# Where the whole-array products of a quad of attention stand: between its scores and its sums

## The reference, cut to what matters

```
x = x + 0.5 * ffn(layernorm(x))          # 8 experts, top 2 of the gate, three ReLU layers of 128x128
x = x + attention(layernorm(x))
x = x + 0.5 * ffn(layernorm(x))          # the same weights again

def attention(x):                        # 16 query heads of 64, ONE key and ONE value head of 64
    q = x @ Wq + bq                      # (8, 512, 16, 64)
    k = x @ Wk + bk;  v = x @ Wv + bv    # (8, 512, 64) each
    w = softmax(q k^T / 8)               # over the 512 keys
    return (w @ v as (8, 512, 1024)) @ Wo + bo
```

## Time and profile before

| | us |
|---|---|
| median of 3 runs (lowest, highest) | 1103.29 (1102.97, 1105.31) |
| the profiled execution, its own time | 1103.85 |
| its span, first to last instruction | 1102.1 |
| TensorE busy | 1040.5 (94%) |
| VectorE, GpSimd, ScalarE busy | 807.5, 693.6, 612.6 |

### The profile page before, as it was taken

The page is one execution under the profiler, slowest core; times in us unless marked ns, Lnnn a source line. Parts: engine busy times, 40 slices in busy tenths (PEclk is TensorE's granted clock), DMA queues, the critical chain, the costliest instruction groups (busy, mean ns, idle before and its releaser), DMA issues.

```text
span 1102.1 us, 15666 instructions
## 1 busy us (share of the span) xinstructions
PE 1040.5 (94%) x5703; PEld 627.2 (57%) x5703; DVE 807.5 (73%) x1023; ACT 612.6 (56%) x867; POOL 693.6 (63%) x370
## 2 busy tenths in 40 slices
PE   4799997679999999999999999999999999998996
PEld 2567885346555655554565555555565455667883
DVE  6879997757756766777587668666577648699994
ACT  4495554436644654564465457457565476675551
POOL 4365556347775786587578567575678666654652
PEclk9899999879999999999999999999999999999998
DMA  5630520000001001000010010001100103513412
GB/s 158 184 105 23 205 101 10 10 1 21 22 23 39 21 22 40 21 21 21 21 40 22 21 40 21 21 21 35 26 21 22 40 23 97 191 58 95 168 47 77
DMA packets 36339, 59.38 MB, mean 54 GB/s; under 512 B 10502, under 2 KB 23847, under 8 KB 36263
## 3 DMA queue, kind: packets, MB, share of 16 engines
q1 hardware_dynamic: 36192, 58.35, 17.6%
q10 hardware_dynamic: 70, 0.02, 0.0%
HBM read 55.20 MB, written 2.62 MB: 52 GB/s over the span
## 4 chain that ended last, share of the span: by engine, by line
PE 84%; DVE 11%; issue 2%; DMA 1%; ACT 1%; POOL 1%; SPq 0%; DVEq 0%; ACTq 0%
PE ring L942 19%; PE ring L680 7%; PE ring L686 6%; PE ring L682 6%; PE ring L895 6%; PE ring L913 5%; PE ring L919 5%; PE ring L915 5%; PE ring L917 5%; PE ring L952 5%; PE ring L928 3%; PE ring L877 2%; DVE ring L1399 1%; PE ring L852 1%; PE ring L878 1%
## 5 line engine op out<-in xcount | busy, mean ns | idle before, releaser
L1566 DVE TENSOR_REDUCE mx<-ring 128x2 f32<-128x1024 f32 x256 | 299.8, 1226 | 92.8 <-PE ring L895 92.8
L575 POOL TENSOR_TENSOR sum_picksT<-sum_picksT,P_wb 128x1024 f32<-128x1024 f32 x128 | 324.5, 2535 | 18.7 <-POOL sum_picksT L575 0.4
L1202 ACT ACTIVATE P_wb<-ring 128x1024 f32<-128x1024 f32 x256 | 262.0, 1027 | 65.1 <-PE ring L919 36.1
L575 POOL TENSOR_TENSOR sum_picksT<-P_wb 128x1024 f32<-128x1024 f32 x64 | 153.8, 2403 | 177.9 <-ACT P_wb L1202 177.9
L618 POOL TENSOR_TENSOR R<-t,R 128x512 fp32r<-128x512 f32 x128 | 164.8, 1310 | 137.9 <-ACT R L1042 137.9
L942 PE MATMUL ring<-P_wb,t 128*64 128x512 f32 x1024 | 226.8, 595 | 0.0
L942 PEld LDWEIGHTS ring<-P_wb,t 128*64 128x64 f32 x1024 | 70.5, 137 | 132.2 <-issue 128.6
L1214 ACT COPY OZ<-ring 128x512 f32<-128x512 f32 x64 | 36.8, 586 | 178.9 <-PE ring L942 133.2
L1037 ACT ACTIVATE t<-ring,bcol 128x512 f32<-128x512 f32 x128 | 81.5, 685 | 96.8 <-PE ring L686 88.1
L680 PE MATMUL ring<-R,whi 128*128 128x512 f32 x320 | 105.1, 410 | 9.4 <-DVE MR L1330 3.7
L895 PE MATMUL ring<-R 64*128 64x512 f32 x512 | 106.9, 415 | 6.2 <-DVE mx L1566 4.0
(11 more groups left out here) (189 smaller groups left out, 1407.2 us busy)
## 6 DMA issues: line engine op xcount, KB each, us to landing
P_wb<-wd SPq DMA_DIRECT2D x64, 512.0 KB, 4.8
rzb_indp<-rzd SPq DMA_DIRECT2D x64, 256.0 KB, 3.9
xs<-in_L_attn_x SPq DMA_DIRECT2D x8, 256.0 KB, 5.0
zrc<-SZ SPq DMA_DIRECT2D x128, 2.0 KB, 1.7
out<-xs SPq DMA_DIRECT2D x8, 256.0 KB, 2.5
sum_picksT<-in_L_ffn_w SPq DMA_DIRECT2D x2, 512.0 KB, 5.1
MR<-mT SPq DMA_DIRECT2D x64, 4.0 KB
t<-in_L_ffn_w SPq DMA_DIRECT2D x1, 512.0 KB, 5.6
```

Source lines behind the costliest of these rows:

```text
L575: pool.tensor_tensor(US[:, g % 2, c, :, :], first, PU[:, TPB * c + t, :, :], ALU.add).then_inc(s_ua, 1)
L1202: act.activation(PU[:, u, :, :], ring[slot(("scores", g, u))][:, :, :], ACT.Exp, scale=SCALE).then_inc(s_exp, 1)
L1566: dve.tensor_reduce(mx[:, :, u], ring[slot(("max", g, u))][:, :, :], AX.X, ALU.max).then_inc(s_max, 1)
```

## The change

Work is reordered; no instruction is added or removed, apart from one use of the ring for the output projection.

1. `turn_max` (whole array) goes ahead of `sums` (32 columns) inside the turn, so that sums and weighing stand next to each other.
2. `x_turn` of the quads i = 1 goes from after the weighing to between q and the turn. For this DVE's `x_normal` moves from quads i = 1 to quads i = 0, and ACT takes the turned x before the sums.
3. The output projection leaves misc of i = 1 and becomes a step "out" of the next quad, i = 2, between q and the turn, with a pair of the ring of its own. ACT's `y_bias` moves with it, ahead of the sums.
4. In g = 31 the first two transposes of the second feed-forward go ahead of the sums.

```diff
@@ misc
-            if i == 1 and b:
-                todo.append(("out", b - 1))
+        def projects(g):
+            return g % QUADS == 2 and g // QUADS > 0
@@ full_steps
-            if misc(b, i) and i != 1:
+            if misc(b, i):
                 steps.insert(0 if i == 2 else len(steps), "misc")
+            if projects(g):
+                steps.append("out")
             if (g, 0) in EARLY:
                 steps.append("gate0")
-            steps.append("turn")
             if g == NQ - 1:
                 steps.append("first_turns")
-            steps.append("weigh")
+            steps += ["turn", "weigh"]
             if (g, 1) in EARLY:
                 steps.append("gate1")
-            if misc(b, i) and i == 1:
-                steps.append("misc")
@@ the ring's uses
+                elif what == "out":
+                    use(("out", g), (s_yb, b))
@@ TensorE, attention
                             banks = ring[slot(("turn", g))]
+                            if g + 1 < NQ:
+                                turn_max(g + 1, banks[:, 1, :])
                             if g:
                                 sums(g - 1, banks[:, 0, :])
-                            if g + 1 < NQ:
-                                turn_max(g + 1, banks[:, 1, :])
...
+                        elif step == "out":
+                            wait_drained(pe, ("out", g))
+                            out_proj(b - 1, ring[slot(("out", g))][:, 0, :])
...
-                            if i == 1 and b:
-                                out_proj(b - 1, misc_bank(g, "out"))
@@ ScalarE, attention
+                    if i == 1 and b + 1 < B:
+                        x_turned(b + 1, misc_bank(g, "x_turn"))
+                    if projects(g):
+                        y_bias(b - 1, ring[slot(("out", g))][:, 0, :])
                     early_gate(g, 0)
-                    if g:
-                        take_sums(g - 1, ring[slot(("turn", g))][:, 0, :])
                     if g == NQ - 1:
                         for b2 in range(2):
                             act.wait_ge(F[1]["xn_transposed"], b2 + 1)
                             act.copy(xh[:, b2, :], ring[slot("first_turns")][:, b2, :]).then_inc(F[1]["x_high"], 1)
+                    if g:
+                        take_sums(g - 1, ring[slot(("turn", g))][:, 0, :])
+                    if g == NQ - 1:
                         root(5)
...
-                    if i == 1 and b + 1 < B:
-                        x_turned(b + 1, misc_bank(g, "x_turn"))
-                    if i == 1 and b:
-                        y_bias(b - 1, misc_bank(g, "out"))
@@ VectorE, attention
-                    if i == 1 and b + 1 < B:
+                    if i == 0 and b + 1 < B:
                         if b + 1 == B - 1:
-                            dve.wait_ge(s_et, TPB)
+                            dve.wait_ge(s_et, TPB - 1)
                         x_normal(b + 1)
```

More of the change, by code:

```diff
@@ L291, in full_steps @@
             steps = ["q"] if g + 2 < NQ else []
-            if misc(b, i) and i != 1:
+            if misc(b, i):
                 steps.insert(0 if i == 2 else len(steps), "misc")
+            if projects(g):
+                steps.append("out")
             if (g, 0) in EARLY:
                 steps.append("gate0")
-            steps.append("turn")
             if g == NQ - 1:
                 steps.append("first_turns")
-            steps.append("weigh")
+            steps += ["turn", "weigh"]
             if (g, 1) in EARLY:
                 steps.append("gate1")
-            if misc(b, i) and i == 1:
-                steps.append("misc")
             return steps
-        MISC_DRAINS = {"out": lambda b: (s_yb, b + 1), "x_turn": lambda b: (s_xtd, b + 1), "k": lambda b: (s_kl, b + 1),
+        MISC_DRAINS = {"x_turn": lambda b: (s_xtd, b + 1), "k": lambda b: (s_kl, b + 1),
                        "v": lambda b: (s_v, b + 1), "y_back": lambda b: (s_ya, b + 1)}
```

## The result

| | before | changed |
|---|---|---|
| median of 5 runs, us | 1102.97 (1102.36 to 1105.31) | 1108.97 (1107.01 to 1110.32) |
| ratio | | 1.0049, 95% interval 1.0035 to 1.0063 |
| span of the profiled execution, us | 1102.1 | 1107.2 |

What follows compares the result with a forecast made beforehand. TensorE was taken to bound the kernel, busy for all but some 4 us of 705 in attention. -2.7 - 1.6 + 0.8 + 1.4 + 3.9 = +1.8 us gave 1105.1 on the median, 8-in-10 range 1100.8 to 1109.

Steps and rivals of the forecast that it cites:

- Part 1, the turn: Turn of the maxima ahead of the sums: two shape changes instead of three, saving 2.7 us, bounds 0 and 5.5.
- B: Rival: going from 32 to 64 columns is free, another 2.7 us saved, 1102.4 us in all; chance 15%.
- Parts 2 and 3: Transposes and output projection moved among whole-array work: 1.6 us saved, bounds 1.0 and 2.0.
- Quads i = 0: Moved x_normal delays ACT's pair, stopping TensorE 0.1 to 0.2 us in g = 4, 8, 12, 16, 24: 0.8 us cost.
- C: Rival: DVE becomes the bound in quads i = 0, each of five stopping 2.4 us; 1110 us; chance 15%.
- the mark: Sign deciding the DVE-bound rival in quads i = 0: scaling ends later than 7.5 us after the weighing's start.
- g = 20: x_normal ahead of the moments delays the first exponential to 11.4 us: 1.4 us cost, bounds 0.5 and 2.5.
- The end: End of attention: POOL's wait for the moved projection delays its additions and the last sums; 3.9 us cost, bounds 1.3 and 5.5.
- what no row shows: Unseen effects, such as a lower clock behind the new idle stretch of the last sums; chance 10%.
- A: Rival: the end is covered, POOL catches up, the 3.9 us is not paid; 1101.2 us; chance 14%.
- The chance of 0.20 for a faster kernel: Chance of a time below 1101.1 us: most of A with B, half of A, and unseen gains.

Runs made afterwards that it cites:

- e1: Changed kernel with POOL's wait for the seventh output projection and its zeroing moved from the end of g=29 between the addition halves of g=30; ratio to kernel before 0.9998.
- e9: Changed kernel with 16 more whole-array products, used by nothing, in front of the last sums to fill TensorE's wait; ratio to the kernel before 1.0036.
- e4: Changed kernel with the last sums (g=31) moved from before layer 1 of unit 1 to behind layer 2 of unit 0; ratio to the kernel before 1.0035.

## Why the prediction came out as it did

The sign was right: 1105.1 was forecast, slower, with 1100.8 to 1109.0 as range; 1108.97 came, 0.03 us inside its upper end. That it lies inside is luck, since the sum was off by more than it forecast: on the profiled execution 1.8 us more was forecast and 5.1 came. The 3.3 us between are, rounded, 1.3 at the end, 1.1 in the quads i = 0, 0.2 in g = 20, 0.3 of gains that did not come in full, and 0.5 of clock in g = 0.

- *Part 1, the turn: 2.7 us.* Right in its unit. q went from 1.59 to 1.50, sums and weighing stayed at 1.00 and 7.02. B, that 32 to 64 columns is free, is refuted by exactly these two numbers. The Trainium skill, page TensorEngine Tiling (Array Packing), section Key Properties, has a drain at every change of mode; the trace agrees in the new direction too.
- *Parts 2 and 3: 1.6 us.* Right: transposes 0.43, projection 6.92 (6.97 in g=30). All gains together are about 4.0 us up to the scores of g=31 (stops of 3.4, a slower start of 0.5, net 0.05), forecast 4.3 with 0.1 of it later.
- *Quads i = 0: 0.8 us.* The mechanism was right, the size was not. I took the stop as pair ready less pair needed, 0.06 to 0.2. It is 0.26 and 0.1 for the restart in g = 5, and 0.34 to 0.41 in each of five: 1.9 us. The first was off because the phase to POOL moved by 0.1, the second was not in the sum at all. C, a whole addition in each quad, did not happen, though the mark that I had set for it did: the scaling ended 7.53 to 7.60 us into the weighing in g = 4, 8, 12 and 16, later than 7.5. The mark was wrong, not only the rival.
- *g = 20: 1.4 us.* 1.55 came, by the way that was forecast: the first exponential came 11.5 us after the weighing's start, forecast 11.4.
- *The end: 3.9 us.* This is the term that was sized worst. That POOL's wait causes it is confirmed by e1. But 5.2 came, because TensorE's 4.4 us of idle time is followed by a stretch at 1.2 GHz; I had left that to what no row shows. With the idle time filled, e9 finds 3.95; that this is my 3.9 is in part luck, for the route was only half right: I held the sums' place in TensorE's list for the cause, and priced DVE's path at 1.3 us as a lower bound. DVE's path is late by 3.6 (the reciprocals), and e4 shows that it stays so whatever the order of TensorE's list. DVE's moments were held four times in the changed kernel (operations of 2.33, 2.30, 2.23 and 2.24 us), where before it was two (2.33 and 2.27).
- A is refuted: POOL did not catch up.
- The chance of 0.20 for a faster kernel is more than its parts: A with B is 0.03 and half of A 0.07, and with the other half of what is unseen it is 0.15.

Sum by the trace: -4.0 + 0.5 + 1.9 + 1.55 + 5.2 = +5.15 us, where the 0.5 at the start is the clock in g=0 and does not belong to the change.

## What to carry to other kernels

When work is moved ahead or back in one engine's list, look for every wait on its semaphore in every other list, above all single ones at the end of a loop: here one `wait_ge` on GpSimd, written for the old place, cost more than 31 quads gained. Long work that is moved also takes its cover with it: list what ran under it at the old place (`x_normal`, ACT's copies), and put that under it at the new one. And a stop of TensorE costs its length plus a restart, 0.1 us here, and it can cost a slower stretch behind it, as it did in each trace here in which the last sums had to wait for some 4 us.

## What the runs showed of the hardware

- Going from 32-column tiles to 64-column tiles costs as much as going to the whole array: sums 1.00 and weighing 7.02 in every order tried.
- The lower clock can also follow shorter stops. The changed kernel, e1, e4 and e9 have the same code in g=21 and the same two stops of TensorE there, 1.6 and 0.7 us. In the changed kernel's trace the clock stays at 1.00 and the scores take 12.5 us; in the other three it falls to 0.50 for a while and they take 14.1. This is e1's clock just behind the first stop, as a mean over 5 us:

```profile
680.00:685.00 5.00, 4.72 (x28) 0.66 0.40 103
```

- A DVE operation on SBUF data that starts during a GpSimd addition is held until that addition ends. Four of the small moments (0.17 us when nothing holds them) took 2.2 to 2.3 us at the end of the changed kernel, and each ended 0.03 to 0.04 us after an addition did (918.32 after 918.28, 920.65 after 920.61, 923.13 after 923.10, 925.61 after 925.58). The longer ones show the same: the scaling took 3.38 us behind `x_normal` in quads i = 0, 1.83 ahead of it, and `x_normal` 3.65 and 5.19. Which of the two is stretched is a matter of order, so the one that others wait for goes first.
